# Quadratic attention with four heads in TensorE's column groups, a Gram matrix for the denominators, and a quarter of the pair products on GpSimd

## The reference, cut to what matters

```python
q = q * scale                                  # scale = 32 ** 0.25
v1 = concatenate([ones, v], axis=-1)           # 33 columns: the first one gives the denominator
qn = _normalize(q) * (scale * temperature)
kn = _normalize(k) * scale
vN = v1 / N
kv_mod = einsum('bhni,bhnj,bhne->bhije', kn, kn, vN)
kv = einsum('bhnd,bhne->bhde', kn, vN)
vsum = sum(vN, axis=-2)
y = 0.5 * einsum('bhni,bhnj,bhije->bhne', qn, qn, kv_mod) + scale**2 * einsum('bhnd,bhde->bhne', qn, kv) + scale**4 * vsum
y_norm, y = (y[..., :1], y[..., 1:])
out = (y / y_norm) @ Wproj.T + bproj
```

## Time and profile before

| | us |
|---|---|
| median of three runs | 2693.18 |
| the profiled execution | 2693.63 |
| its span (first to last instruction) | 2691.9 |
| normalization and queries, 0 to 113.2 | 113.2 |
| first tile of the moment loop, up to its feature matmuls | 14.0 |
| moment loop, 127.2 to 288.8 | 161.6 |
| turn between the passes | 24.8 |
| answers, 313.6 to 571.2 | 257.6 |
| graph network and experts | 2120.7 |

### The profile page before, as it was taken

The page is one execution under the profiler, slowest core; times in us unless marked ns, Lnnn a source line. Parts: engine busy times, 40 slices in busy tenths (PEclk is TensorE's granted clock), DMA queues, the critical chain, the costliest instruction groups (busy, mean ns, idle before and its releaser), DMA issues. The chain is left out here.

```text
span 2691.9 us, 42091 instructions
## 1 busy us (share of the span) xinstructions
PE 2499.2 (93%) x13717; PEld 1663.6 (62%) x13717; DVE 1593.9 (59%) x3109; ACT 700.6 (26%) x1454; POOL 1359.3 (50%) x1412
## 2 busy tenths in 40 slices
PE   4899899979999999789999998899999994999998
PEld 3533445547555555675555556755555673899997
DVE  6789777736566666456566664567788887011111
ACT  2312100022121221421222224122222230554443
POOL 0000230007777777377777773777777730344443
PEclk7899799989999999999999998999999996999999
DMA  4500387535455544445555554534445422133331
GB/s 113 182 1 1 119 287 246 188 115 159 137 162 162 162 150 148 143 141 158 162 152 163 161 154 127 177 116 142 146 147 147 129 81 100 33 96 96 67 67 31
DMA packets 197271, 354.43 MB, mean 132 GB/s; under 512 B 28217, under 2 KB 152196, under 8 KB 196967
## 3 DMA queue, kind: packets, MB, share of 16 engines
q0 software_dynamic: 66864, 167.97, 22.6%
q1 hardware_dynamic: 126274, 180.06, 20.1%
q10 hardware_dynamic: 3956, 4.19, 0.6%
HBM read 286.04 MB, written 66.61 MB: 131 GB/s over the span
## 5 line engine op out<-in xcount | busy, mean ns | idle before, releaser
L1515 POOL DMA_INDIRECT xnT<-h_rows,idx x780 | 777.1, 996 | 237.8 <-issue 218.1
L1140 PEld LDWEIGHTS g_pagg<-g_onehot,xnT 128*128 128x128 f16 x4680 | 330.8, 98 | 225.2 <-issue 209.0
L1515 POOL DMA_INDIRECT xnT<-xn_rows,idx x366 | 365.7, 999 | 130.2 <-issue 103.0
L1140 PE MATMUL g_pagg<-g_onehot,xnT 128*128 128x144 f16 x4680 | 385.5, 227 | 23.6 <-DMA xnT<-h_rows,idx 16.1
L1357 DVE TENSOR_TENSOR g_agg<-g_agg,g_pagg 128x288 f32 x585 | 265.3, 453 | 113.1 <-PE g_pagg L1140 57.7
L1360 DVE SCALAR_TENSOR_TENSOR g_onehot<-iota_keys,shift,keys 128x288 f16<-128x288 f16 x585 | 299.2, 513 | 0.6 <-DVE g_pre_at L1349 0.6
L1449 DVE SCALAR_TENSOR_TENSOR g_t<-g_ph,g_bh,g_rz 128x448 f32<-128x448 f32 (+1 forms) x144 | 90.0, 625 | 307.2 <-PE g_ph L1217 290.0
L1309 ACT ACTIVATE g_nT<-g_t,g_bi 128x448 f32<-128x448 f32 (+1 forms) x144 | 89.5, 622 | 579.7 <-DVE g_t L1456 573.1
L1968 DVE TENSOR_TENSOR f_ys<-f_bank,f_b 128x256 f32<-128x256 f32 x53 | 22.5, 425 | 341.9 <-PE f_bank L1923 270.2
L1217 PE MATMUL g_pr<-g_agg,g_wc 128*128 128x448 f32 (+1 forms) x576 | 218.9, 502 | 4.1 <-DVE g_agg L1357 4.0
L1217 PE MATMUL g_pr<-g_hT,g_wh 128*128 128x448 f32 (+1 forms) x576 | 219.5, 504 | 0.0
(11 more groups left out here) (359 smaller groups left out, 3329.0 us busy)
## 6 DMA issues: line engine op xcount, KB each, us to landing
ma_R<-q_cols SPq DMA_DIRECT2D x27, 896.0 KB, 10.4
f_w<-in_L_ffn_W SPq DMA_DIRECT2D x16, 1024.0 KB, 8.1
h_cols<-g_hn SPq DMA_DIRECT2D x36, 448.0 KB
h_rows<-g_rows SPq DMA_DIRECT2D x36, 448.0 KB
g_hT<-h_cols SPq DMA_DIRECT2D x36, 448.0 KB, 5.8
mix_R<-q_cols SPq DMA_DIRECT2D x15, 896.0 KB, 10.0
xnT<-h_rows,idx POOLq DMA_INDIRECT x780
ma_R<-q_cols SPq DMA_DIRECT2D x9, 1120.0 KB, 5.9
```

The costliest lines, as they stand in the source:

```text
L1140: mm = e.matmul(pg[:, k * TYPES:(k + 1) * TYPES, :].rearrange("p t d -> p (t d)"), rows[:, c, o:o + P], hot[:, c, :], start=(c == 0 and pa ...
L1515: e.indirect_dma_start(ring[:, b % SLABS, c, :], None, tables[s], bass.IndirectOffsetOnAxis(ap=idx[:, o:o + 1], axis=0)).then_inc(landed[b ...
```

## The change

The moments: the values lose their column of ones. Four heads lie side by side, at PSUM partitions 0, 32, 64 and 96. The 16 diagonals 1 to 16 of a head are 512 features; the squares, the plain keys and a one are 65 more. GpSimd forms a quarter of the 512-wide products (`pair_features(e, i, 1, 1)`), VectorE the other three quarters in three instructions of 1024 elements. The denominator comes from a Gram matrix of the keys, two matmuls of 129 columns a tile. The turn transposes 12 blocks instead of 36 and the tables go.

The answers: a block of four turned copies is made for four diagonals and 32 channels at once on 128 partitions, so that one unit has 16 matmuls of 32 columns, four beside each other, instead of 16 full ones; the loads go from four to eleven DMAs a unit (eight of them read one row for four partitions). The denominators are 4 matmuls with 4 columns, inverted on 112x16 elements and spread again by ScalarE and 4 matmuls; the answer is finished one unit later than before. In unit 0 GpSimd forms two of the four blocks.

```diff
+def load_turned(e, X, q_cols, u, landed):
+    q = q_cols[u % KC]
+    def rows(turn, head, dims):
+        return bass.AP(q.tensor, q.offset + (QUAD * turn + head) * NP + u // KC * GW, dims + [[1, GW]])
+    e.dma_start(X[:, SELF, :], rows(0, 0, [[NP, P]])).then_inc(landed[0], 16)
+    for h in range(QUAD):
+        e.dma_start(X[:, AHEAD8 + h, :], rows(8, h, [[QUAD * NP, HD], [0, 4]])).then_inc(landed[1], 16)
+    e.dma_start(X[:, TURN:TURN + QUAD, :], rows(9, 0, [[QUAD * NP, HD], [QUAD * NP, 4], [NP, QUAD]])).then_inc(landed[2], 16)
+    e.dma_start(X[:, TURN4:TURN4 + QUAD, :], rows(13, 0, [[QUAD * NP, HD], [QUAD * NP, 4], [NP, QUAD]])).then_inc(landed[3], 16)
+    for h in range(QUAD):
+        e.dma_start(X[:, STAY + h, :], rows(0, h, [[QUAD * NP, HD], [0, 4]])).then_inc(landed[4], 16)
...
+def products(e, X, E, b):
+    still = AHEAD8 if b < 2 else STAY
+    turned = (TURN, TURN4)[b % 2]
+    return e.tensor_tensor(paired(X, E, b), X[:, still:still + QUAD, :], X[:, turned:turned + QUAD, :], ALU.mult)
...
@@ mix_moments, GpSimd
-                e.memset(shared[:, :], 0.0).then_inc(S["zero"], 1)
+                for i in range(KTILES):
+                    e.wait_ge(S["wrap"], i + 1)
+                    if i >= 2:
+                        e.wait_ge(S["mm"], i - 1)
+                    pair_features(e, i, 1, 1).then_inc(S["feat_last"], 1)
+                for p in (1, 3, 4):
+                    e.wait_ge(r_in[p], LANDED[p])
+                for b in (1, 3):
+                    products(e, K["R0"], K["E0"], b)
@@ mix_moments, TensorE
+                    for m in range(KC):
+                        e.matmul(pm[3][:, m * (P + 1):(m + 1) * (P + 1)], kt_all[i % 2][0:n, m, 0:P], kt_all[i % 2][0:n, m, :], ...)
+                    for m in range(KC):
+                        for h in range(QUAD):
+                            e.matmul(pm[2][HD * h:HD * (h + 1), m * REST:(m + 1) * REST], vf[i % 3][0:n, QUAD * m + h, :], F[i % 2][0:n, QUAD * m + h, FD:PAIRED], ...)
+                    for m in range(KC):
+                        e.wait_ge(S["feat"], KC * i + m + 1)
+                        if m == 1:
+                            e.wait_ge(S["feat_last"], i + 1)
+                        for h in range(QUAD):
+                            mm = e.matmul(pm[m][HD * h:HD * (h + 1), :], vf[i % 3][0:n, QUAD * m + h, :], F[i % 2][0:n, QUAD * m + h, 0:FD], ...)
@@ mix_moments, VectorE
-                    features(i, 0)
-                    features(i, 2)
+                    features(i, 0, 0)
+                    features(i, 0, 1).then_inc(S["feat"], 1)
                     if i + 1 < KTILES:
                         inverse(i + 1)
-                    features(i, 4)
-                    if i + 1 < KTILES:
                         extend(i + 1)
-                    features(i, 6)
+                    features(i, 1, 0).then_inc(S["feat"], 1)
@@ mix_answers, TensorE, unit u
+                def pair_block(u, b):
+                    f = paired(R[u % RING], pairs[u % 2], b)
+                    for h in range(QUAD):
+                        mm = e.matmul(py[u % 2][HD * h:HD * (h + 1), :], K["Wq"][:, u % KC, b, HD * h:HD * (h + 1)], f[:, h, :], ...)
+                def spread(u):
+                    e.wait_ge(S["wide"], u + 1)
+                    for t in range(4):
+                        mm = e.matmul(pinv[:, t * PT:(t + 1) * PT], wide[:, t, :, :].rearrange("p h e -> p (h e)"), ident[0:PT, 0:PT], start=True, stop=True)
...
+                    e.matmul(py[u % 2][:, :], K["W2"][:, m, 1, :], q, ...)
+                    e.matmul(pz[:, :], K["T"][:, m, :], q, start=True, stop=True).then_inc(S["z"], 1)
+                    e.matmul(py[u % 2][:, :], K["W2"][:, m, 0, :], square[u % 2][:, :], ...)
+                    pair_block(u, 0)
+                    pair_block(u, 1)
+                    if u >= 3 and u % 2:
+                        project((u - 3) // 2)
+                    if u:
+                        spread(u - 1)
+                    pair_block(u, 2)
+                    pair_block(u, 3).then_inc(S["y"], 1)
+                    for t in range(4):
+                        mm = e.matmul(pden[:, t * QUAD:(t + 1) * QUAD], G[:, t * PT:(t + 1) * PT], K["same_head"][:, :], start=True, stop=True)
@@ mix_answers, VectorE, unit u
+                    e.scalar_tensor_tensor(out=G[:, :], in0=pz[:, :], ...)
+                    pair(u + 1, 0)
+                    pair(u + 1, 1)
+                    final(u - 1)
+                    pair(u + 1, 2)
+                    pair(u + 1, 3)
+                    if u >= 3 and u % 2:
+                        add((u - 3) // 2)
+                    e.tensor_scalar(den[:, :], pden[:, :], 16 * SC ** 4, None, ALU.add).then_inc(S["inv"], 1)
+                    e.reciprocal(inv[:, :], den[:, :]).then_inc(S["inv"], 1)
```

More of the change, by code:

```diff
@@ L215, in mix_moments @@
         ext = [sb(f"ext{b}", [P, HEADS, HD + HD // 2]) for b in range(2)]
[L216 to L220, removed]
+        room = sb("F", [P, 2 * HEADS * PAIRED])
+        F = [room[:, b * HEADS * PAIRED:(b + 1) * HEADS * PAIRED].rearrange("p (h f) -> p h f", h=HEADS) for b in range(2)]
+        vf = [sb(f"vf{b}", [P, HEADS, HD]) for b in range(3)]
+        kt_all = [sb(f"keys{b}", [P, KC, P + 1]) for b in range(2)]
+        sums, small = sb("sums", [P, KC, FD]), sb("small", [P, KC, 2, P])
         stats, mv = sb("stats", [PT, TILES, 6]), sb("mv", [PT, TILES, 2])
@@ new lines, in _ @@
+                e.wait_ge(S["sums"], 2 + 2 * KC)
+                for m in range(KC):
+                    for k in range(2):
+                        mm = e.transpose(pm[4][:, (2 * m + k) * P:(2 * m + k + 1) * P], small[:, m, k, :], ident[:, :])
+                mm.then_inc(S["turned"], 1)
+                for m in range(KC):
+                    for b in range(BLOCK):
+                        mm = e.transpose(pkv[m][:, b * P:(b + 1) * P], sums[:, m, b * P:(b + 1) * P], ident[:, :])
+                    mm.then_inc(S["turned"], 1)
@@ L798, in mix_answers @@
+def mix_answers(nc, A, acc, ident, q_cols, K, acc_rows, idx0, rows_from, ring, landed):
     with ExitStack() as ctx:
@@ L817, in mix_answers, with turned_in @@
         py = [ps(f"py{b}", [P, GW]) for b in range(2)]
-        pz, pden = ps("pz", [P, GW]), ps("pden", [P, GW])
+        pz, pinv = ps("pz", [P, GW]), ps("pinv", [P, GW])
+        pden = ps("pden", [PT, 4 * QUAD])
         po = [ps(f"po{b}", [PT, 2, C]) for b in range(2)]
-        S = {n: sem(f"ma_{n}") for n in ("in", "T", "same", "small", "feat", "square", "z", "G", "den", "den_out", "inv", "y", "final", "po", "added", "parked")}
-        r_in = [[sem(f"ma_r_in{i}{p}") for p in range(len(PIECES))] for i in range(RING)]
+        S = {n: sem(f"ma_{n}") for n in ("in", "small", "feat", "square", "z", "G", "den", "inv", "wide", "spread", "y", "total", "final", "po", "added", "parked")}
+        r_in = [[sem(f"ma_r_in{i}{p}") for p in range(PARTS)] for i in range(RING)]
+        def turned_in(e, u, *parts):
+            for p in parts:
+                e.wait_ge(r_in[u % RING][p], LANDED[p] * (u // RING + (u % RING > 0)))
         with nc.Block() as block:
```

362 lines of the change are left out of this document (154 added, 208 removed).

## The result

The changed kernel takes 2607.61 us (median of four runs, 2605.75 to 2608.89) against 2694.65 (four runs, 2691.22 to 2696.93) before: ratio 0.9677, 95% interval 0.9661 to 0.9694. The profiled execution has a span of 2606.8 us, 85.1 less than before's. The forecast was 2605; A's 2557 and D's 2789 are far off. Whole times come from several chips, on which the unchanged graph network takes from 2121 to 2366 us; so they are compared as ratios to the kernel before on the same chip, or stage by stage.

The account below looks back on a forecast made before the run. TensorE was taken to bound the answers, TensorE and VectorE nearly full in the moment loop, waits the turn. Moment loop +8, turn -12, answers -84.6 gave -88.6 on 2693.6: 2605 us, range 2550 to 2640.

Parts of the forecast that it names:

- A: Rival, moment loop and turn: GpSimd runs beside VectorE without blocking; -137 us, 2557 in all; chance 0.22.
- D: Rival, whole change: waits drop TensorE to 1.2 GHz, so the kernel gets slower, 2789 us; chance 0.04.
- Moment loop: Tile of 4.8 us work plus 2.1 blocking by GpSimd, 6.9 against 6.56: +8 us over 24 tiles.
- nearly whole, 2.1: Moment loop: of GpSimd's product, taken as 2.3 us (bounds 0.9 and 2.6), 2.1 blocks VectorE in every tile.
- The turn: Between moment loop and answers: from 24.8 us to 12.9 with GpSimd blocking, 9.7 without; -12 or -15.
- GpSimd starts about a us before the sums end: Turn: GpSimd's two products for unit 0, 4.0 us each, would hold VectorE's first product there until 7.
- Answers: Loads bind, 10.95 us a unit; stage 167 plus 6 for coupling, 173 against 257.6: -84.6 us.
- 15.5 behind the last one: End of answers after the last load: 6.5 us through the denominators, then 9 for spreading, `final`, projection and addition.
- What was costed at nothing: The part before the moment loop, and the unchanged graph network and experts after the answers: each forecast to move 0.
- B: Rival, moment loop and answers: only two column groups overlap; answers gain 65 us, 2625 in all; chance 0.11.
- C: Rival, answers: replicating loads run at 300 GB/s, 205 us instead of 173; 2637 in all; chance 0.09.
- E: Rival, moment loop: GpSimd's product takes far over 2.6 us; at 5 us, +71 and 2668 in all; chance 0.04.

Follow-up runs that it names:

- experiment 1: Changed kernel with GpSimd's two products for unit 0 waiting until VectorE has formed the last tile's features; 2595.26 us, ratio 0.9636.
- Experiment 3: As experiment 1, VectorE forming three quarters of the moment loop's features, GpSimd's quarter left out (zero); 2560.73 us, tiles of 4.96 us.
- experiments 1 to 4: Three have their own lines; the second is experiment 1 with all moment-loop features formed on VectorE, none on GpSimd: 2581.4 us, ratio 0.9575.
- the last of 9: All features and unit 0's products on VectorE, the latter at the answers' start; end reordered, gathers held until late in the answers; 2566.85 us, ratio 0.9539.
- experiment 4: As Experiment 3, with GpSimd writing 3072 zeros a partition to unused memory in each tile; 2548.63 us, tiles of 4.96 us.
- experiment 7: All features on VectorE; in the answers heads 2 and 3 write to the column groups of heads 0 and 1: two units 26.3 us, answers 201.5.

## Why the prediction was right, point by point

The mechanisms were right: four column groups overlap, the loads become the bound of the answers, GpSimd's product holds VectorE's, the turn shrinks by half or more. That the sum came within 3 us is luck: its five terms were off by -4.4, -9.6, -4.3, +7.2 and +14.6 us, which cancel to 3.5.

**Moment loop: sign wrong.** Forecast tiles of 6.9, +8 us; measured 6.19, -8.9 us for 24 tiles, and 7.9 lost at the end. The mechanism (GpSimd's product holds VectorE's) was right. Mis-sized was how much of it: "nearly whole, 2.1". By itself GpSimd's product takes 2.06 us, not 2.3; its record of 2.77 is above the upper bound of 2.6 only by the 0.7 that it waits for VectorE's product, which costs VectorE nothing. Of the 2.06, some 0.35 lie beside the sum of squares and 1.7 are holding; the forecast named 0.4 of that kind, but 2.3 less 0.4 is 1.9 and not the 2.1 it used. The other 0.3 of the miss is VectorE's sum: 4.8 forecast, 6.19 - 1.7 = 4.5 measured. TensorE's 4.8 measured 4.96 where it alone binds. The 8.9 are counted from a mean of 6.56. In the trace before, tiles alternate between 6.25 and 6.81, and the "undisturbed" 6.24 of the prediction is every second one; against that one the tile of 6.19 is no gain. What lengthened the others stays open.

**The turn: right chain, wrong time for GpSimd.** "GpSimd starts about a us before the sums end" failed: nothing in its queue made it wait for the end of the loop, and it started 13.8 us before (269.00 against 282.84). The price fell in the loop, on VectorE's last features. Without it, barrier included, the turn was forecast at 9.7 and measured 8.5; with it, in experiment 1, 11.1 from the end of the sums, against 12.9.

**Answers: the loads, yes; the end, no.** The forecast's terms were 2 + 149.6 for the loads, 15.5 behind the last one, 6 of coupling. Measured: 152.5 up to the last landing (at 382 GB/s where the engines are full, forecast 377), so nothing of the 6 there, and 27.7 behind it. The failed term is the 15.5. Its first part, 6.5 up to the last denominators, measured 13.8 (443.8 to 457.6): the two products end at 449.2, but ahead of the last two blocks there stand, on TensorE's queue, the projection of the group before (5.1, from 448.74) and a spreading (1.1), which the sum left out. Its second part, 9, measured 13.9: the last projection was priced at 5.1, the row at the upper clock, but takes 9.6 at 1.2 GHz, 4.5 more. Experiment 3 has the same code of the answers, and there the clock stayed at its upper level to the end (timeline, then the stretch with columns as in the earlier trace rows):

```profile
418.63 0.17 DVE L980 TENSOR_SCALAR ma_den<-ma_pden 112x16 f32<-112x16 f32 x1 [0.70 <-PE ma_pden L910]
418.60:427.60 9.00, 6.34 (x28) 3.95 (x28) 2.39 (x5) 1.15 (x2) 0.00 (x0) 1.00 0.18 51
```

From the last denominators to the end it is 9.0 us at a clock of 1.00: the sum of this part was right for the clock it was priced at. The last projection took 9.4, 7.1, 5.2 and 8.0 us in experiments 1 to 4, and the clock fell 2.1, 1.2 and 2.4 us behind the last denominators in 1, 2 and 4, and not before the end in 3. So this term is worth 5.2 to 9.6 from run to run; what decides where the clock falls stays open. Unit and bounds: 10.75 on the mean for 11.3; TensorE 10.2 for 9.9, VectorE 10.35 for 10.5, loads 10.75 for 10.95.

**What was costed at nothing.** The part before the loop moved by -4.4. The loop's first projection starts 1.8 us earlier (111.53 for 113.28), within the 109.6 to 113.1 us of the later traces. The other 2.7 lie between it and the first feature matmul: 11.3 us for 13.9, and 9.2 to 11.2 in the later traces. The scaling that the earlier trace rows shows stretched is short again (0.17 for 0.95), the clock rose earlier, and TensorE's first feature matmul waits for two of VectorE's products, where that of the kernel before waited for all four, to 127.08:

```profile
125.80 1.28 DVE L731 TENSOR_TENSOR mk_F<-mk_ext 128x1088 f32<-128x1088 f32 x1
```

How the 2.7 divide was not tried. The rest of the program, unchanged, took 2120.7 us before and, on comparable chips, 2135.3, 2126.5, 2132.1, 2131.4, 2121.0 and 2129.9 in the traces of the changed kernel and of experiments 1 to 4 and the last of 9. TensorE's instructions between 600 and 1080 us (before's time) stand 99.5 us earlier after the change, those from 1200 to 1600 97.5, from 1760 to 2190 95.6, from 2240 to the end 85.5: whole steps of the graph network are alike, and the 14 us are lost at their joints. What makes a joint longer or shorter stays open; it was not tried, and experiment 4, with 2121.0, shows that the change does not force it. Without this term the forecast would have been 11 us too high instead of 3 too low.

**The rivals.** A (no holding) fell: 1.7 us a tile. B fell with experiment 7. C fell: 382 GB/s, eight replicating DMAs included. D fell: clock 0.95 in the loop, at a TensorE busy 80%; the lower level came for 3 us at the loop's start, from 271.4 (while TensorE waited for the last features) through the turn, in four stretches of 3 to 14 us in the answers up to 363.5, and from 459.1 on. E fell: 2.77 us, waiting included.

## What to carry to other kernels

Before work is moved from VectorE to GpSimd, look which instruction of VectorE will stand beside it: here a product on GpSimd held VectorE for longer than VectorE would have needed for the same product. Give an engine that runs ahead a wait that ties its next work to the phase in which it is meant to run; with its inputs long there, it starts early and holds others where it is least wanted. Where three resources are within a few per cent, price the start and the end of the stage by their own queues and clock: the 12 us missed here behind the last load were a projection left out of the sum and a clock that fell. Read a long record against what runs on the other engine: part of it can be waiting.

## What the runs showed of the hardware that was not expected

- A GpSimd instruction that only writes left VectorE's two-input products alone (2.36 us beside a memset of 2.66) but held an 8-element scaling in place to its end (0.43 for 0.16); GpSimd's product did the reverse of the first (4.03 for 2.36).
- The holding went both ways: GpSimd's product took 2.37, 2.77 and 3.23 us when VectorE's had 0.28, 0.72 and 1.18 us to go, and 2.06 by itself.
- VectorE stayed held over two GpSimd products that follow each other without a gap (269.00 and 272.92, 3.95 us each): three products of the last tile ended behind both, 7.9 us late, the first of them with a record of 11.04 us.
- The unchanged graph network takes 2121 to 2135 us on one group of chips and 2338 to 2366 on others, while the loop and the turn of one and the same code agree within 0.1 us on all of them.
- The same code of the answers takes 173.2 to 180.2 us; up to 4.4 of it is the last projection, at 5.2 us or at 9.6, by the clock that was granted.
